# First filter step with its spectral products in six PSUM banks, its threshold partly on ScalarE, and the third pair whitened inside it

## What is computed

```python
# whitening: covariance of all tokens, Cholesky, inverse
ff = (1 - EPS) * (f @ f.T / (n - 1)) + EPS * eye(c)
x  = (solve_triangular(cholesky(ff), eye(c)) @ f) * gamma + beta     # f = x - mean
residual = x
h = layer_norm(x, n1_g, n1_b)                                        # LN1
xf = rfft2(h, axes=(1, 2), norm='ortho')                             # per image
o1 = relu(complex_block_matmul(xf, w1) + b1)                         # layer 1
o2 = softshrink(complex_block_matmul(o1, w2) + b2, 0.01)             # layer 2
h = irfft2(o2) + h + residual
residual = h
h = gelu(layer_norm(h, n2_g, n2_b) @ mw1 + mb1) @ mw2 + mb2          # LN2, MLP
return h + residual
# softshrink(v, lam): v - sign(v) * lam where |v| > lam, else 0
```

## Time and profile before

| | |
|---|---|
| median of 3 runs | 765.5 us (762.21 to 769.13) |
| profiled execution | 769.99 us, span 768.2 us |
| mean granted TensorE clock | 0.961 of full |
| PE busy | 713.0 us, 93% |
| DVE busy | 567.5 us, 74% |
| ACT busy | 389.4 us, 51% |
| POOL busy | 276.4 us, 36% |
| DMA queue q1 | 38.20 MB, 17.0% of 16 engines |

### The profile page before, as it was taken

One profiled execution on the slowest core, in us unless ns is written; L12 is line 12 of the kernel. 1 busy time (PEld: TensorE's weight loads), 2 busy tenths in 40 slices (PEclk: granted clock), 3 DMA queues, 4 the chain that ended last, 5 costly groups with the idle time before them and its releaser, 6 DMA issues.

```text
span 768.2 us, 29376 instructions
## 1 busy us (share of the span) xinstructions
PE 713.0 (93%) x12889; PEld 453.6 (59%) x12889; DVE 567.5 (74%) x1845; ACT 389.4 (51%) x709; POOL 276.4 (36%) x158
## 2 busy tenths in 40 slices
PE   6998999787789999999999999999999989989897
PEld 5886557756556656665666656565656555545443
DVE  4466997948698958986897789688968896852661
ACT  0012003652375747664766576656656555746365
POOL 7000000573374064607540654156324723471000
PEclk9899999976989999999999999999999999989999
DMA  9954000302000310040003000300000010000011
GB/s 258 273 147 145 3 2 2 87 2 60 29 3 15 110 33 20 20 117 27 16 26 110 27 15 26 110 27 15 27 26 27 15 39 26 27 14 31 25 44 60
DMA packets 11088, 40.07 MB, mean 52 GB/s; under 512 B 1954, under 2 KB 2082, under 8 KB 9506
## 3 DMA queue, kind: packets, MB, share of 16 engines
q1 hardware_dynamic: 10962, 38.20, 17.0%
HBM read 25.35 MB, written 12.85 MB: 50 GB/s over the span
## 4 chain that ended last, share of the span: by engine, by line
PE 62%; DVE 24%; ACT 8%; issue 5%; DMA 1%; POOL 0%; DVEq 0%; ACTq 0%
PE psum L1222 8%; PE psum L1213 8%; PE psum L1189 7%; DVE stats L630 6%; ACT o_g L1426 6%; PE psum L1143 4%; PE psum L891 4%; PE psum L1095 3%; PE psum L1111 3%; DVE hbuf L691 3%; PE psum L942 3%; PE psum L1202 3%; PE psum L1231 3%; PE psum L1157 2%; DVE oslice L749 2%
## 5 line engine op out<-in xcount | busy, mean ns | idle before, releaser
L1449 ACT ACTIVATE hid<-psum,hbias 128x448 f32<-128x448 f32 x224 | 124.7, 635 | 66.2 <-PE psum L1213 66.2
L1213 PE MATMUL psum<-n2T,mw1s 64*128 64x448 f32 x448 | 105.4, 582 | 6.9 <-ACT o_g L1426 6.1
L442 POOL TENSOR_TENSOR hbuf<-hbuf,prm 128x896 f32<-128x896 f32 (+1 forms) x29 | 53.6, 1848 | 160.7 <-PE psum L1095 160.7
L1222 PE MATMUL psum<-hid,prm 128*64 128x448 f32 x448 | 96.3, 552 | 4.9 <-DVE oslice L749 4.7
L463 POOL TENSOR_TENSOR p_y<-layer,clamped 128x512 f32<-128x512 f32 (+1 forms) x64 | 75.9, 1185 | 55.1 <-DVE clamped L740 55.1
L437 POOL TENSOR_TENSOR rbuf<-ybuf,prm 128x512 f32<-128x512 f32 (+2 forms) x10 | 32.4, 3238 | 163.8 <-DVE hbuf L863 129.2
L1458 ACT ACTIVATE mlp_t<-psum,prm 128x448 f32<-128x448 f32 x56 | 35.5, 635 | 60.1 <-PE psum L1222 58.6
L1157 PEld LDWEIGHTS psum<-cst,p_y 58*64 58x64 f32 x2048 | 51.2, 135 | 22.3 <-issue 21.6
L1157 PE MATMUL psum<-cst,p_y 58*64 58x112 f32 x2048 | 61.1, 265 | 2.9 <-ACT o_g L1432 2.9
L1213 PEld LDWEIGHTS psum<-n2T,mw1s 64*128 64x128 f32 x448 | 40.1, 190 | 38.0 <-issue 24.9
L1189 PE MATMUL psum<-o_g,cst 58*128 58x448 f32 x256 | 55.6, 554 | 1.1 <-ACT o_g L1432 1.1
(11 more groups left out here) (140 smaller groups left out, 1342.7 us busy)
## 6 DMA issues: line engine op xcount, KB each, us to landing
xin<-x_dram SPq DMA_DIRECT2D x8, 1568.0 KB, 8.8
out_dram<-oslice SPq DMA_DIRECT2D x112, 112.0 KB
ybuf<-x_dram SPq DMA_DIRECT2D x2, 1568.0 KB, 16.7
fbuf<-x_dram SPq DMA_DIRECT2D x2, 1568.0 KB, 19.5
xin<-x_dram SPq DMA_DIRECT2D x4, 392.0 KB, 5.4
n<-x_dram SPq DMA_DIRECT2D x1, 1568.0 KB, 22.6
n<-x_dram SPq DMA_DIRECT2D x4, 392.0 KB, 14.6
prm<-params_dram SPq DMA_DIRECT2D x1, 646.0 KB, 4.1
```

The source lines that it names most:

```text
L442: nc.gpsimd.tensor_tensor(h4[:, j0:j1], h4[:, j0:j1], gain[:, j0:j1].unsqueeze(2).broadcast_to((RP, j1 - j0, W, 2)), ALU.mult).then_inc(h_ ...
L1213: nc.tensor.matmul(t[:, 0:4 * ROWS], mw1s[C * v:C * v + C, HH * m:HH * m + HH], n2T[C * v:C * v + C, s % 2, :], start=True, stop=True).the ...
L1222: last = nc.tensor.matmul(t[C * v:C * v + C, 0:4 * ROWS], pp("mw2")[:, C * m:C * m + C], hid[:, s % 2, m, v, :], start=(m == 0), stop=(m = ...
L1449: nc.scalar.activation(hid[:, s % 2, m, v, :], bank[CH_MLP[i].bank[k]][:, 0:4 * ROWS], ACT.Gelu, bias=hbias[:, m:m + 1]).then_inc(c_act, 1)
```

## The change

Five edits, all in the order and the placing of work:

1. **Six banks in step 0.** In step 0 alone `layer_2` and `inv_w` write to three pairs of banks, (6,7), (4,5), (1,2) in turn, instead of banks 1 and 2 (`spectral_bank`, `free_spectral`).
2. **Threshold partly on ScalarE in step 0.** DVE still adds the bias, into one of three buffers lent by `hid`. Its clamp is gone; ACT writes relu(-v - 0.01) and relu(v - 0.01) instead, and POOL subtracts the one from the other (`shrink_first`).
3. **Third pair in step 0.** The transposes of pair 2 go between the `dft_w` products, and pair 2 is whitened in step 0, between the chunks of `layer_2`, in banks 0 and 3. Step 1 whitens nothing.
4. **LN1 ahead of the folded weights.** PE's `folded_weights` goes behind `inv_w`, and DVE's behind LN1 of pair 1.
5. **First MLP input in two orders.** For slice 0 of pairs 0 to 6 the second half of the hidden units (m = 1) goes first; PE issues it ahead of `whiten_two(1)`, and waits for all of `layer_1` only ahead of m = 0. ACT takes `ev_n2` ahead of the last chunk of `layer_1`.

The diff, cut to its core:

```diff
-    return BANK_M if i == 1 and k % 2 == 1 else BANK_X
+    return BANK_M if 0 < i < 3 and k % 2 == 1 else BANK_X
+THIRD_WHITEN = (BANK_X, BANK_M, BANK_X, BANK_M, BANK_X, BANK_M, BANK_X)
+FIRST_SPECTRAL = ((1, 2), (6, 7), (4, 5))
+def spectral_bank(i, k):
+    return FIRST_SPECTRAL[(k - L2) // 2 % 3][k % 2] if i == 0 else B_BANK[k]
+def hid_order(i, s):
+    return (1, 0) if s == 0 and not last_pair(i) else (0, 1)
...
+        def shrink_bufs(i, c):
+            if i == 0:
+                spare = hid[:].rearrange("p s m v n -> p (s m v n)")
+                return [spare[:, 512 * j:512 * j + 512] for j in (c % 3 * 2, c % 3 * 2 + 1)]
+            return [layer2[:, c % L2_BUFS, :], clamped[:, c % L2_BUFS, :]]
...
                 def ev_layer_2(i, cs):
-                        if c >= L2_BUFS or i > 0:
-                            dve.wait_ge(y_ready, i * 8 + c - L2_BUFS + 1)
+                        bufs = 3 if i == 0 else L2_BUFS
+                        if c >= bufs or i > 0:
+                            dve.wait_ge(y_ready, i * 8 + c - bufs + 1)
...
+                        if i == 0:
+                            continue
                         dve.wait_ge(b_dve, i * B_DVE + b_done("dve", L2 + c))
-                        nc.vector.tensor_scalar(clamped[:, c % L2_BUFS, 0:n], layer2[:, c % L2_BUFS, 0:n], LAM, -LAM,
+                        nc.vector.tensor_scalar(bound[:, 0:n], value[:, 0:n], LAM, -LAM,
...
+                def first_step():                       # VectorE
+                    ev_layer_1(0, L1_DVE)
+                    ev_whiten(2, [0])
+                    ev_layer_2(0, [0, 1, 2, 3])
+                    ev_whiten(2, [1, 2])
+                    ev_layer_2(0, [4, 5])
+                    ev_whiten(2, [3, 4])
+                    ev_layer_2(0, [6, 7])
+                    ev_whiten(2, [5, 6])
+                    mean_rstd(1, 0)
+                    for k in range(2):
+                        ln1_subtract(1, k)
+                        ln1_rstd(1, k)
+                    folded_weights()
+                    ev_inv_h(0, range(8))
+                    for k in range(4):
+                        ln2_stats(0, k)
...
+                def free_spectral(i, k):
+                    if i > 0:
+                        return free_b(i, k)
+                    if L2 + 6 <= k < INVW:
+                        pe.wait_ge(b_dve, b_done("dve", k - 6))
+                    if k >= INVW + 6:
+                        pe.wait_ge(b_act, b_done("act", k - 6))
+                    return bank[spectral_bank(i, k)]
...
+                def first_step():                       # TensorE
+                    transpose_x(2, [0, 1])
+                    dft_w(0, 0)
+                    transpose_x(2, [2, 3])
+                    dft_w(0, 1)
+                    transpose_x(2, [4, 5])
+                    dft_w(0, 2)
+                    transpose_x(2, [6])
+                    layer_1(0, [0])
+                    dft_w(0, 3)
+                    layer_1(0, [2, 4, 6])
+                    whiten(2, [0])
+                    pe.wait_ge(b_act, b_done("act", L2 - 1))
+                    pe.wait_ge(b_dve, b_done("dve", L2 - 1))
+                    layer_2(0, 0, range(L2_KH[0]))
+                    layer_2(0, 1, range(L2_KH[1]))
+                    layer_2(0, 2, range(L2_KH[2]))
+                    whiten_two(2, 0)
+                    layer_2(0, 3, range(L2_KH[3]))
+                    whiten_two(2, 1)
+                    whiten_two(2, 2)
+                    for k in range(4):
+                        inv_w(0, k, range(4))
+                    folded_weights()
+                    for k in range(4):
+                        inv_h(0, k)
+                    for q in range(4):
+                        dft_h(1, q)
...
                     whiten_next(0)
 
+                    if behind:
+                        pe.wait_ge(b_act, i * B_ACT + b_done("act", L1 + 2))
+                        pe.wait_ge(b_dve, i * B_DVE + b_done("dve", L1 + 3))
+                        mlp_in(i - 1, 0, (1,))
+                    whiten_next(1)
                     pe.wait_ge(b_act, i * B_ACT + b_done("act", L2 - 1))
                     pe.wait_ge(b_dve, i * B_DVE + b_done("dve", L2 - 1))
                     if behind:
                         mlp_in(i - 1, 0, (0,))
-                    whiten_next(1)
-                    if behind:
-                        mlp_in(i - 1, 0, (1,))
                         transpose_n(i - 1, 1)
                     whiten_next(2)
...
+                def shrink_first(c):                    # ScalarE
+                    n = L2_KH[c // 2] * C
+                    over, under = (m[:, 0:n] for m in shrink_bufs(0, c))
+                    act.wait_ge(b_dve, b_done("dve", L2 + c))
+                    nc.scalar.activation(under, over, ACT.Relu, bias=minus_lam[:], scale=-1.0)
+                    nc.scalar.activation(over, over, ACT.Relu, bias=minus_lam[:]).then_inc(shrunk, 1)
+                def first_step():
+                    ev_x(2, [0, 1])
+                    ev_dft_w(0, [0, 1])
+                    ev_x(2, [2, 3])
+                    ev_dft_w(0, [2, 3])
+                    ev_x(2, [4, 5])
+                    ev_dft_w(0, [4, 5])
+                    ev_x(2, [6])
+                    ev_layer_1(0, [0])
+                    ev_dft_w(0, [6, 7])
+                    ev_layer_1(0, range(1, 8))
+                    for c in range(8):
+                        shrink_first(c)
+                    ev_inv_w(0, range(8))
+                    for q in range(4):
+                        ev_dft_h(1, q)
...
-                    ev_layer_1(i, range(1, 8))
+                    ev_layer_1(i, range(1, 6))
                     if behind:
                         ev_n2(i - 1, 0)
+                    ev_layer_1(i, [6])
```

72 lines of the change are left out of this document (33 added, 39 removed).

## The result

| | before | after |
|---|---|---|
| median | 767.7 us (762.21 to 770.67, 12 runs) | 759.95 us (753.67 to 763.56, 12 runs) |
| profiled execution | 769.99 us, span 768.2 us | 759.7 us, span 757.7 us |
| mean granted clock | 0.961 | 0.975 |
| PE, DVE, ACT, POOL busy | 713.0, 567.5, 389.4, 276.4 us | 703.4, 564.7, 396.9, 278.2 us |

The ratio of after to before is 0.9894, with a 95% interval of 0.9867 to 0.992. That is 8.1 us less, between 6.1 and 10.2. The forecast was 9.9 us less for the profiled execution (760.1; it took 759.7) and 756 for the median. The same program measured once more (experiment 9) gave 0.9874. Of the 56 further runs of the kernel before, taken beside the experiments, one of 774.73 us was in a slower state of the chip and is left out in what follows.

The account below looks back on a forecast made before the run. PE and DVE were taken to set the pace together in steady steps, a bare chain of waits in step 0. 5.9 + 2.0 + 0.5 + 1.5 = 9.9 us took the median from 765.5 to 756 us, range 748 to 762.

Parts of the forecast that it names:

- Up to the second layer: Step 0 until T, the start of layer_2: pair 2's transposes and evacuations make T 0.4 us later, between 0 and 2.5.
- The threshold: Step 0, layer_2 to inv_w: pipelined over DVE, ACT and POOL, last subtraction at T + 13.5 instead of 16.6, gain 3.1 us.
- The rule on relu and VectorE: Skill page's rule to put relu, min and max on VectorE; by it step 0's threshold would be slower than before.
- The inverse transforms: Step 0, inv_w up to inv_h: three bank pairs leave one wait, 9.9 us instead of 13.1, gain 3.2 (0 to 4.6).
- Step 0 in sum: Step 0: -0.4 + 3.1 + 3.2 = 5.9 us gained, bounds 0 and 8.5.
- Head of step 1: Up to layer_2 of step 1: m = 1 done while DVE still works; gain 2.0 us, 3.3 at best, 0.5 at half clock.
- Steady steps: Heads of steps 2 to 6: DVE's second LN2 product held behind POOL's add_h; 0.5 us in five steps (-0.5 to 2).
- Head of step 7: Up to layer_2 of step 7: m = 1 fills PE's wait for ACT; 1.5 us, 0.6 if the clock falls, 2.6 if not.
- the first rival: Step 0 and head of step 1 stay at half clock, leaving 2.2 us of gain: 763 us; chance 0.14.
- All heads gain: Full clock in step 0, gains at every step's head, 0.4 us in each steady step: 16.4 us, so 749; chance 0.18.
- ACT was not too slow: Rival: ACT too slow for step 0's threshold, from 1.6 us a pair nothing won there: 759 us; chance 0.07.
- the changed kernel was not slower: Rival: the clock stays low into step 1; 18 us of low clock would give 781 us; chance 0.03.

Follow-up runs that it names:

- experiment 9: The changed kernel measured once more, nothing altered: 757.61 us, ratio 0.9874 to the kernel before.
- experiment 1: Kernel before plus only the new order of the first MLP input (m = 1 first, ACT's ev_n2 earlier): 764.06 us, ratio 0.9981.
- Experiment 7: Changed kernel with DVE's adds of chunks 4 and 5 in step 0 ahead of the whitening evacuations: 762.53 us, ratio 0.9943 to the kernel before.
- experiment 4: Changed kernel with layer_2 and inv_w of step 0 in banks 1 and 2 again: 772.45 us, ratio 1.0057 to the kernel before.
- experiment 8: Changed kernel plus thirteen idle PE products in step 0, nine of them ahead of inv_w: 758.19 us, ratio 0.9874 to the kernel before.
- experiment 6: Changed kernel with the last two of POOL's four add_h parts left out for pairs 1 to 7: 757.18 us, one run.
- experiment 2: Changed kernel with the old order of the first MLP input, all else kept: 760.91 us, ratio 0.9931 to the kernel before.
- experiments 5: Kernel before with the last two of POOL's four add_h parts left out for pairs 1 to 7: 767.62 us, one run.

## Why the prediction was right, step by step

The time was right, and the sum nearly so, but in part by luck: terms were off in both directions, and the clock helped. The two profiles differ by 10.5 us of span. The stretches of the forecast give 5.2 + 2.9 + 0.3 + 2.7 = 11.1 where it had 9.9; the part up to S took 1.1 us longer, and the part from step 7's `layer_2` on 0.5 less. The forecast worked from an execution near the slow end of the runs before (769.99, of 762.21 to 770.67), in which the clock was at half for 17 us of step 0's threshold and inverse transforms. It took these half-clock lengths as what the code costs. Between the medians the gain is 8.1 us.

- **Up to the second layer** (forecast: T 0.4 us later). From S to T the profile after has 16.16 us, the one before 16.59: 0.4 earlier. Over the five profiles of the same code it is 15.89 to 16.46. The seven evacuations fitted into ACT's open time, and PE was at full clock, where before it was at 0.79. In experiment 1, the code before at a clock of 0.89 here, the same stretch took 15.17 us. So the transposes do cost 0.7 to 1.3 us, about as forecast or more, and the clock hid it.
- **The threshold** (3.1 us). 1.7 us: `inv_w` starts at T + 14.90 instead of T + 16.64. Over the five profiles it is T + 12.90 to T + 14.90. But T + 16.64 was itself at half clock. The code before starts `inv_w` at T + 14.40 when the clock is full up to 175.6 us (experiment 1), so against that the change wins 1.0 to 1.5 us here with one standstill, and with two it is 0.2 to 0.5 us later. The 3.1 us counted the old round trips at 3.93 us, and they are 3.28 at full clock. The pieces were right: a pair of ACT passes takes 1.2 us, the lower of the two values, and four subtractions 5.00. What failed was "six chunks at once, and DVE, ACT and POOL work as a pipeline". DVE's queue puts whitening evacuations between the adds of chunks 3 and 4, and I counted their time but not what they wait for. When PE is late with the whitening, the adds behind stand still too. Experiment 7 shows the order's part (T + 12.50 with the same standstills), experiment 9 the standstills' part (T + 13.15).
- **The rule on relu and VectorE**, from the Trainium skill ("ScalarE: Activation LUTs", Rules for kernel authors), did not hold here: with the clamp on DVE the threshold ends 0.37 us later, not earlier, and the ratio of the whole kernel was 0.0051 worse. ACT's part is still not the whole of the term. The banks decide more: without them the last subtraction ends 4.9 us later (experiment 4), though that is with the whitening between the chunks and at a lower clock.
- **The inverse transforms** (3.2 us). 3.0 us: 10.09 us from the start of `inv_w` to that of `inv_h`, where 9.9 was forecast and 13.13 was before. In the profile after, the first 5.3 us of it ran at half clock; at full clock it is 7.67 (experiment 8), 5.5 less than before, so the bound of 4.6 in the prediction was too low. Its other bound, 0 for all at half clock, was too high: four products of 3.2 and 1.3 make 14.1, 1 us more than before. This is the surest of the terms: the code before gives 13.12 to 13.18 in three profiles, the changed one 9.50 to 10.53 in five. DVE's margin of 0.2 us was right: LN1 and the folded weights end at 194.27, and the first add of `inv_h` waits 0.16 us for PE. With `inv_w` any faster, DVE is the bound, as experiments 7 and 8 show.
- **Step 0 in sum** (5.9 us; the bounds of its terms add up to -0.1 and 8.2, where 0 and 8.5 were given). 5.2 us between the two profiles (53.80 and 48.59). Over all profiles of each code it is 50.32 to 53.82 before (three) and 46.19 to 48.79 after (five), means 52.65 and 47.28: 5.4 us. The 50.32 is experiment 1, with the clock at half for 10 us from S on instead of 24; against it the mean of the five leaves 3.0 us, all of them in the inverse transforms. So between 3 and 5.4 us of step 0 are the change's own, and whether the change also keeps the clock up there, as the profiles suggest (7 to 10 us at half instead of 24 in two of the three before), is not shown.
- **Head of step 1** (2.0 us, between 0.5 and 3.3). From E to `layer_2` it is 28.57 us instead of 31.47: 2.9, with the clock at half from 204.9 to 215.1 but full in the last 13 us. That is a lucky profile. In eight of the ten profiles with the new step 1 and edit 5 the clock fell in the last 9 us ahead of `layer_2` and it took 29.58 to 30.11 us (30.09 in experiment 6), a gain of 1.4 to 1.9; in experiment 9 it took 27.65. Without edit 5 it is 30.02 (experiment 2), no more. So as far as these profiles tell, the typical gain comes from the whitening that has left, and the waits that edit 5 fills show as a gain only where the clock stays up.
- **Steady steps** (0.5 us in five). 0.26, within the scatter. Experiments 1, 2, 5 and 6 show the mechanism as forecast: L701 cannot run beside POOL's `add_h`. By the Trainium skill's rule of a lock held for a whole instruction ("SBUF — State Buffer", SBUF: two separate sides) the steps give 0. The trace agrees: L701 starts at 302.33 but ends only at 304.84, 1.89 us behind POOL's last part (302.95), which is nearly the whole 2.02 that it takes alone. I had expected L701 to be unable to move at all. It does start earlier, and its time grows by what it has to wait, 2.02 to 2.51 us.
- **Head of step 7** (1.5 us, between 0.6 and 2.6). 2.7 between the two profiles. Of these 1.4 to 2.0 are whether the clock fell, since the old order had pitches of 72.02 and 72.68 us with the clock full (experiments 5 and 2); 0.5 to 1.3 are edit 5's.
- **The rivals.** The clock did take part of the gain behind the threshold, as the first rival said, but not in the first half. "All heads gain" failed at the steady steps. ACT was not too slow. The clock came back within `inv_w`, and the changed kernel was not slower.

What is not settled is why PE stands still for 0.8 to 1.8 us where the profile shows no releaser. It happens at the same few places in differing number, and in the kernel before too (0.89 us at 155.29, in `dft_w`). I took no standstill away, so the cause is open.

## What to carry to other kernels

When an in-order engine serves a pipeline and side work together, cost each side job by when its input comes, not only by how long it takes; the work queued behind inherits that wait. Where every pair of PSUM banks costs a round trip between engines, side work put into the round trips makes them longer; here it paid with six banks and lost with two. Before taking a stage's length as what its code costs, look at the granted clock in it, and at a second profile: the same threshold took 16.64 us at half clock and 14.40 at full. A time won on one of two engines that set the pace together is lost again at the next place where they meet, so look for that place (here a product of two SBUF tensors beside POOL) before counting it.

## What the runs showed that I had not expected

- One program's span goes with its mean granted clock, about 4 us for each 0.01 over its runs, and the same wait (2.14 us ahead of the last MLP) is followed by eight products in 1.77 us in one profile and 3.30 in another.
- PE stood still for about a microsecond with no releaser within dense runs of small products, once or twice in the same places of the same program; with the second the threshold ended 1.6 us later.
- A DVE product of two SBUF tensors and a POOL operation exclude each other in both directions: DVE's grows from 2.02 to 2.51 us when POOL is first, and POOL's subtraction from 1.29 to 3.00 when DVE is.
- Thirteen idle products made step 0 some 1.5 us shorter (means of 45.8 over three profiles and 47.28 over five), and the medians of three kernels with such products did not fall below that of the kernel without.
